# Who evacuates the transposed probabilities: one PSUM copy in two moved from ScalarE to VectorE, and the layer-norm pieces drained two heads later

## The chip, the cores and the metric

The kernel runs on all 8 cores of one Trainium2 chip. Each core takes one of the 8 batch entries; the cores exchange nothing. The metric is the device time of the slowest core in microseconds (us).

## What is computed

One post-layer-norm transformer layer on x of shape (8, 2048, 1024): windowed attention (16 heads of 64, causal, window 512) with a layer norm on every head's q and k, then an 8-bit quantized linear layer, each with a residual and a layer norm.

```python
qkv = x @ W_qkv + b_qkv                      # split into q, k, v; 16 heads of 64
q, k = layernorm(q, gq, bq), layernorm(k, gk, bk)   # per head
scores = q @ k.T / 8
scores = where((col > row) | (row - col >= 512), -inf, scores)
attn = softmax(scores) @ v
x1 = layernorm(x + attn @ W_out + b_out)
n  = x1 * rsqrt(mean(x1**2) + 1e-6)
q8 = clip(round(n * s), -128, 127) / s       # s = 127 / max|n|
out = layernorm(x1 + q8 @ (w_int8 * weight_scale).T + bias)
```

## The kernel before, in words

Each core works on 2048 rows in 16 tiles of 128 rows. All weights stay on the chip. A software pipeline of 21 rounds (`r`, `NR = NT + 5`) does in round r: the q, k and v projections of tile t = r, the attention of tile a = r-2, the output projection of tile p = r-3, the quantized layer of tile f = r-4, and the elementwise chains that follow p (as `pc = r-4`) and f (as `fc = r-5`). So rounds 2 and 3 have attention and no chains, round 4 has attention and the first chain only, rounds 5 to 17 have attention and both chains, and in rounds 16 and 17 the projections of q, k and v have ended.

Every engine runs its own list of instructions strictly in the order in which the program appended them (`S_.plan[engine]`); engines meet only at semaphores: `W(engine, sem, val)` appends a wait, `INC` an operation that counts a semaphore up when it is done. `FDV` (L172) and `FAC` (L176) append a one-column copy on VectorE and on ScalarE, called "fence" in the profile, whose end is what other engines wait for.

The attention of a tile is done in two halves of 8 heads (`attn_half`, half 0 with heads 0 to 7, half 1 with heads 8 to 15). Between the halves stand the k projection and, on VectorE, the normalization of q (L759 to L766), the statistics of k (L349 to L368) and the copy of the transposed keys into `kfm` (L786). For head h the program appends, in this order:

- `stage_scores` of h: TensorE multiplies q by the keys (L413 to L425) into one of two PSUM buffers, `big0` or `scp`; VectorE takes a maximum over 64 columns (L437, `negC`) and a fence; ScalarE takes the exponential (L444, `probs`); GpSimd multiplies it by the mask (L450).
- `stage_transpose` of h-2: TensorE transposes up to five 128x128 blocks of `probs` into the single PSUM buffer `ptp` (L186), which is then copied to `probsT`. This evacuation is done by VectorE for even heads (`pt_evac`, L196) and by ScalarE for odd heads (L465, followed by a fence). `G["ptev"]` remembers who evacuated last: the next transposes into `ptp` wait for it.
- `stage_av` of h-4: TensorE multiplies `probsT` by v into `avp` (L485); ScalarE copies the result to `araw` (L498). The single buffer `avp` makes each of these wait for the copy before it.
- `drain_chain(1)`: one piece of the elementwise chains.

After head 15 the two last transposes and the last four products follow, then VectorE divides by the sums (L524, L529).

The chains are lists of pieces in `pending_chain`. That of `pc` has seven: t1 (row sum, L551), t2 (sum of squares and small operations, L556 to L564, and the ScalarE square root chain), t3 (L582), t4 (L592 to L597), t5 (small operations, L605 to L619), t6 (L625 to L630) and t7 (L634 to L642). That of `fc` has four: ta (L652, L654), t1' and t2' (the same as t1 and t2) and tb (L663, and the store of the tile on the SyncE queue). In a round from 5 on there are thus 11 pieces, handed out one per head, and heads 11 to 15 have none. A piece stands in VectorE's list behind the head's maximum and evacuation and ahead of the next head's maximum.

Of the kernel before, what the change touches and what calls it, by code (L numbers as in the profile page):

```python
# [12 lines left out]
AF = mybir.ActivationFunctionType  # L13
# [16 lines left out]
class Sched:  # L30
# [13 lines left out]
    def W(self, eng, sem, val):  # L44
        if val and val > 0:
            h = self.sem[sem]
            self.trace[eng].append(("w", sem, val))
            self.plan[eng].append(lambda e, h=h, v=val: e.wait_ge(h, v))  # L48
# [14 lines left out]
    def INC(self, eng, sem, fn, k=1):  # L63
        self._self_edge(eng)
        self.cnt[sem] += k
        h = self.sem[sem]
        self.trace[eng].append(("i", sem, k))
        self.plan[eng].append(
            lambda e, fn=fn, h=h, k=k: fn(e).then_inc(h, k))
        return self.cnt[sem]  # L70
# [17 lines left out]
def build_nc():  # L88
# [19 lines left out]
    with st:  # L108
# [53 lines left out]
        ptb = ptp.ap()  # L162
# [4 lines left out]
        W, OP, INC = S_.W, S_.OP, S_.INC  # L167
        G = {"ptev": ("sDV", 0), "sqr": 0, "sqf": 0, "rysq": 0, "rsv": 0,
             "big0": 0, "big0k": "sDV", "big1": 0, "big1k": "sDV"}
# [5 lines left out]
        def FAC():  # L175
            return INC("scalar", "sAC", lambda e: e.activation(  # L176
                out=fence.ap()[:, 1:2], in_=cst.ap()[:, 0:1], func=AF.Square))
# [16 lines left out]
        def pt_evac(dst_ap, w, vPE):  # L194
            W("vector", "sPE", vPE)
            v = INC("vector", "sDV", lambda e, a=dst_ap, w=w: e.tensor_copy(  # L196
                out=a, in_=ptb[:, 0:w]))
            G["ptev"] = ("sDV", v)
            return v

        vS_const = 0
        for dst, src in [(mask4.ap(), d["mask4"]), (ident.ap(), d["ident"]),
# [8 lines left out]
            out=wqkv.ap().rearrange("p (k n) -> p k n", n=3 * E),  # L211
            in_=d["wqkv"].rearrange("(k p) n -> p k n", p=128)), 16)
        vG_wout = INC("gpsimd", "sWO", lambda e: e.dma_start(
            out=wout.ap().rearrange("p (k n) -> p k n", n=E),
# [238 lines left out]
        def stage_transpose(aa, h, vPL_m):  # L453
            u = aa * H + h
            nblk, w, _, _ = attn_geom(aa)
            pb = probs[u % 4].ap()
            vPE = transpose_group(
                lambda c, pb=pb: pb[:, c * 128:(c + 1) * 128],
                nblk, [("sPL", vPL_m)], "pT")
            vPE_tr_u[u] = vPE  # L460
            dst = probsT[u % 4].ap()[:, 0:w]
            if u % 2 == 1:
                W("scalar", "sPE", vPE_av_u.get(u - 4, 0))
                W("scalar", "sPE", vPE)
                INC("scalar", "sAC", lambda e, dst=dst, w=w: e.activation(  # L465
                    out=dst, in_=ptb[:, 0:w], func=AF.Copy))
                v = FAC()
                G["ptev"] = ("sAC", v)
                vDV_pt_u[u] = ("sAC", v)
            else:  # L470
                W("vector", "sPE", vPE_av_u.get(u - 4, 0))
                vDV_pt_u[u] = ("sDV", pt_evac(dst, w, vPE))
            expPEgate[u + 4] = vPE

        def stage_av(aa, h):
# [25 lines left out]
        def attn_half(aa, half):  # L501
            if half == 0:
                W("tensor", "sDV", vDV_qfm[aa])
                W("tensor", "sDV", vDV_kfm[aa])
                W("tensor", "sDV", vDV_vev[aa])
                G["attn_pend"] = []
            pend = G["attn_pend"]
            for h in range(8 * half, 8 * half + 8):
                m = stage_scores(aa, h)
                pend.append((h, m))  # L510
                if len(pend) >= 3:
                    hh, mm = pend.pop(0)
                    stage_transpose(aa, hh, mm)
                    if hh >= 2:
                        stage_av(aa, hh - 2)
                drain_chain(1)
            if half == 1:
                for hh, mm in pend:
                    stage_transpose(aa, hh, mm)
                for hh in range(H - 4, H):  # L520
                    stage_av(aa, hh)
                W("vector", "sAC", last_avev[aa * H + H - 1])
                a3 = araw.ap().rearrange("p (h c) -> p h c", c=65)
                INC("vector", "sDV", lambda e, a3=a3: e.reciprocal(  # L524
                    out=rcp[aa % 2].ap()[:, 0:16], in_=a3[:, :, 64:65]))
                rb_ = rcp[aa % 2].ap().rearrange(
                    "p (h u) -> p h u", u=1).broadcast_to([128, 16, 64])
                vno = INC("vector", "sDV", lambda e, a3=a3, rb_=rb_, aa=aa:
                          e.tensor_tensor(  # L529
                    out=attn[aa % 2].ap().rearrange("p (h c) -> p h c", c=64),  # L530
                    in0=a3[:, :, 0:64], in1=rb_, op=ALU.mult))
                G["anorm"] = vno
                vAC_attn_done[aa] = vno
# [3 lines left out]
        def drain_chain(n=None):  # L537
            k = len(pending_chain) if n is None else min(n, len(pending_chain))
            for _ in range(k):
                pending_chain.pop(0)()  # L540
# [418 lines left out]
```

How the kernel before makes its waits and increments, by code:

```python
    def W(self, eng, sem, val):  # L44
        if val and val > 0:
            h = self.sem[sem]
            self.trace[eng].append(("w", sem, val))
            self.plan[eng].append(lambda e, h=h, v=val: e.wait_ge(h, v))
# [14 lines left out]
    def INC(self, eng, sem, fn, k=1):  # L63
        self._self_edge(eng)
        self.cnt[sem] += k
        h = self.sem[sem]
        self.trace[eng].append(("i", sem, k))
        self.plan[eng].append(
            lambda e, fn=fn, h=h, k=k: fn(e).then_inc(h, k))
        return self.cnt[sem]
```

## Time and profile before

| what | value |
|---|---|
| time, median of 2 runs | 1887.78 us (1887.53 to 1888.02) |
| the profiled execution, its own time | 1885.52 us |
| its span on the slowest core (core 1) | 1883.8 us (all cores 1878.4 to 1883.8) |
| busy: TensorE, VectorE, ScalarE, GpSimd | 44%, 51%, 27%, 18% of the span |
| mean granted TensorE clock | 0.66 of full speed |

The profile is of one execution. The timeline gives for each instruction its start and its duration in us, and in brackets how long its engine had been idle and which engine's operation ended that. Line numbers are those of the kernel before.

### The profile page before, as it was taken

Reading aid. Unit: us, or ns where it says so; the run is one execution under the profiler, and the core shown is the slowest. Engines: PE = TensorE matmul, PEld = TensorE weight load, DVE = VectorE, ACT = ScalarE, POOL = GpSimd, SP = SyncE. Lnnn points to the kernel's source line nnn. Section 1 sums busy time; section 2 is a strip of 40 time slices with the busy share of each in tenths; the row PEclk is TensorE's granted clock in tenths of the full one; section 3 lists DMA queues with packets and bytes.
Section 4 is the critical chain, followed back from the end, with each engine's and each line's share of the span. In section 5 each row is a group of like instructions: output and inputs, shape, how many; then the busy total and the mean of one; then the engine's idle time right before and its main releaser. Section 6 shows DMA issues by size and latency. Waiting matters only on the chain.

```text
span 1883.8 us, 21143 instructions; the slowest of 8 cores (1878.4 to 1883.8 us)
## 1 busy us (share of the span) xinstructions
PE 833.7 (44%) x5096; PEld 428.0 (23%) x5096; DVE 965.8 (51%) x1873; ACT 511.8 (27%) x1105; POOL 336.5 (18%) x281
## 2 busy tenths in 40 slices
PE   0134555354444545344453543545454354444521
PEld 0021222121222222122322322232122222232300
DVE  2126553727455472744647365473736537455355
ACT  0001322322334132332413233241333324242311
POOL 0000111112213021221302122130222213132200
PEclk9996766666575756657575665757566575656565
DMA  9420000000101000010000101000010000000000
GB/s 153 91 67 6 1 6 6 12 6 1 29 1 29 1 7 23 1 29 1 25 4 1 28 1 29 1 23 6 1 28 1 23 1 23 1 23 1 23 11 23
DMA packets 11808, 35.11 MB, mean 19 GB/s; under 512 B 1322, under 2 KB 1450, under 8 KB 11690
## 3 DMA queue, kind: packets, MB, share of 16 engines
q0 software_dynamic: 4480, 12.59, 4.4%
q1 hardware_dynamic: 7210, 21.17, 3.3%
q8 instruction: 46, 0.75, 0.2%
q14 instruction: 72, 0.59, 0.1%
HBM read 37.97 MB, written 8.39 MB: 25 GB/s over the span
## 4 chain that ended last, share of the span: by engine, by line
DVE 45%; PE 25%; ACT 12%; issue 11%; DMA 3%; DVEq 2%; another core or an unknown queue 2%; ACTq 1%; POOL 0%; SPq 0%; POOLq 0%
PE big L331 7%; PE big L828 5%; PE ptp L186 4%; ACT probs L444 4%; PE big L858 3%; ACT probsT L465 3%; DMA rci<-w 2%; DVE probsT L196 2%; DVE fence L172 2%; DVE zzb L349 2%; DVE arena L359 2%; DVE negC L437 2%; DVE arena L351 2%; DVEq L48 2%; PE avp L485 2%
## 5 line engine op out<-in xcount | busy, mean ns | idle before, releaser
L450 POOL TENSOR_TENSOR probs<-probs,mask4s 128x640 bf16<-128x640 bf16 (+4 forms) x256 | 323.6, 1264 | 1285.2 <-ACT probs L444 1282.2
L186 PE MATMUL ptp<-idents,probs 128*128 128x128 bf16 x1120 | 160.3, 302 | 490.0 <-ACT fence L176 189.7
L331 PE MATMUL big<-wqkvb,xfm 128*128 128x512 bf16 x768 | 216.1, 445 | 58.3 <-DVE vtm L722 33.9
L186 PEld LDWEIGHTS ptp<-idents,probs 128*128 128x128 bf16 x1120 | 100.0, 129 | 575.9 <-issue 575.4
L828 PE MATMUL big<-woutb,afm 128*128 128x512 bf16 x256 | 91.6, 522 | 119.8 <-DVE afm L196 119.8
L444 ACT ACTIVATE probs<-scp,negC 128x640 bf16<-128x640 f32 (+4 forms) x128 | 93.0, 727 | 185.3 <-DVE fence L172 163.7
L485 PE MATMUL avp<-vtm,probsT 128*128 128x65 bf16 x1120 | 108.4, 243 | 60.8 <-ACT araw L498 57.6
L331 PEld LDWEIGHTS big<-wqkvb,xfm 128*128 128x128 bf16 x768 | 82.9, 112 | 179.9 <-issue 124.8
L356 ACT ACTIVATE sqqk<-zzb 128x1024 bf16<-128x1024 bf16 x32 | 33.8, 1057 | 318.3 <-DVE zzb L349 318.3
L196 DVE COPY probsT<-ptp 128x640 bf16<-128x640 bf16 (+4 forms) x128 | 57.6, 450 | 114.1 <-PE ptp L186 104.2
L444 ACT ACTIVATE probs<-big,negC 128x640 bf16<-128x640 f32 (+4 forms) x128 | 93.0, 727 | 63.7 <-DVE fence L172 53.4
L485 PEld LDWEIGHTS avp<-vtm,probsT 128*128 128x128 bf16 x1120 | 82.5, 129 | 83.5 <-issue 82.1
L870 ACT ACTIVATE hb<-big,lar 128x1024 f32<-128x1024 f32 x16 | 17.8, 1113 | 291.6 <-PE big L858 291.6
L465 ACT ACTIVATE probsT<-ptp 128x640 bf16<-128x640 bf16 (+4 forms) x128 | 81.5, 636 | 42.6 <-PE ptp L186 30.7
L349 DVE CAST zzb<-big 128x1024 bf16<-128x1024 f32 x32 | 39.2, 1225 | 89.6 <-PE big L338 88.2
L838 DVE TENSOR_TENSOR hb<-big,xres 128x1024 f32<-128x1024 f32 x16 | 19.6, 1225 | 110.6 <-PE big L832 110.6
L858 PE MATMUL big<-wfT,q8fm 128*128 128x512 bf16 x256 | 59.7, 387 | 37.4 <-DVE q8fm L196 37.4
L498 ACT ACTIVATE araw<-avp 128x65 bf16<-128x65 f32 x256 | 57.9, 226 | 59.8 <-PE avp L485 40.2
L172 DVE COPY fence<-cst 128x1 f32<-128x1 f32 x352 | 54.2, 154 | 37.9 <-DVE negC L437 2.1
L413 PE MATMUL big<-kfm,qfm 64*128 64x512 bf16 (+3 forms) x80 | 39.1, 489 | 71.2 <-ACT probs L444 70.8
L828 PEld LDWEIGHTS big<-woutb,afm 128*128 128x128 bf16 x256 | 28.8, 122 | 171.0 <-issue 162.4
L722 DVE CAST vtm<-big 128x512 bf16<-128x512 f32 x32 | 22.2, 694 | 68.8 <-PE big L338 66.9
(120 smaller groups left out, 1315.6 us busy)
## 6 DMA issues: line engine op xcount, KB each, us to landing
xres<-x SPq DMA_DIRECT2D x16, 512.0 KB, 4.5
out<-x1b SPq DMA_DIRECT2D x16, 512.0 KB, 2.9
wqkvb<-wqkv POOLq DMA_DIRECT2D x1, 6144.0 KB, 43.9
rci<-w SPq DMA_DIRECT2D x16, 256.0 KB, 2.8
xbf<-x POOLq DMA_DIRECT2D x16, 256.0 KB, 4.3
woutb<-wout POOLq DMA_DIRECT2D x1, 2048.0 KB, 56.0
mask4s<-mask SPq DMA_DIRECT2D x1, 160.0 KB
idents<-ident SPq DMA_DIRECT2D x1, 32.0 KB
```

What stands on the lines that cost most here:

```text
L172: return INC("vector", "sDV", lambda e: e.tensor_copy(out=fence.ap()[:, 0:1], in_=cst.ap()[:, 0:1]))
L186: fn = lambda e, src=src, c=c: e.transpose(ptb[:, c * 128:(c + 1) * 128], src, ident.ap())
L196: v = INC("vector", "sDV", lambda e, a=dst_ap, w=w: e.tensor_copy(out=a, in_=ptb[:, 0:w]))
L331: OP("tensor", lambda e, l=lhs, r=rhs, ps=ps, kk=kk: e.matmul(ps, l, r, start=(kk == 0), stop=False))
L349: vDV_cp = INC("vector", "sDV", lambda e, b=bigap: e.tensor_copy(out=zzb.ap(), in_=b))
L444: scb=scb: e.activation(out=pb[:, 0:w], in_=scb.ap()[:, 0:w], func=AF.Exp, bias=dstC, scale=1.0))
L450: e.tensor_mul(pb[:, 0:w], pb[:, 0:w], mask4.ap()[:, moff:moff + w]))
L465: INC("scalar", "sAC", lambda e, dst=dst, w=w: e.activation(out=dst, in_=ptb[:, 0:w], func=AF.Copy))
L485: fn = lambda e, pT=pT, j=j, vb=vb, last=(j == nblk - 1): e.matmul(avp.ap()[:, 0:65], pT[:, j * 128:(j + 1) * 128], vtm.ap()[:, vb:vb + 65 ...
L498: e.activation(out=dstA, in_=avp.ap()[:, 0:65], func=AF.Copy))
L828: OP("tensor", lambda e, l=l, rr=rr, n=n, kk=kk: e.matmul(big1.ap()[:, n * 512:(n + 1) * 512], l, rr, start=(kk == 0), stop=False))
L858: fn = lambda e, l=l, rr=rr, n=n, kk=kk: e.matmul(big1.ap()[:, n * 512:(n + 1) * 512], l, rr, start=(kk == 0), stop=(kk == NCH - 1))
```

## The change

Every evacuation of `ptp` into `probsT` is now done by VectorE, for odd heads as for even ones; ScalarE's copy and the fence behind it are gone for odd heads. And a piece of the chains is handed out only from head 2 of a tile on (`h` counts from 0 to 15 over both halves).

```diff
             dst = probsT[u % 4].ap()[:, 0:w]
-            if u % 2 == 1:
-                W("scalar", "sPE", vPE_av_u.get(u - 4, 0))
-                W("scalar", "sPE", vPE)
-                INC("scalar", "sAC", lambda e, dst=dst, w=w: e.activation(
-                    out=dst, in_=ptb[:, 0:w], func=AF.Copy))
-                v = FAC()
-                G["ptev"] = ("sAC", v)
-                vDV_pt_u[u] = ("sAC", v)
-            else:
-                W("vector", "sPE", vPE_av_u.get(u - 4, 0))
-                vDV_pt_u[u] = ("sDV", pt_evac(dst, w, vPE))
+            W("vector", "sPE", vPE_av_u.get(u - 4, 0))
+            vDV_pt_u[u] = ("sDV", pt_evac(dst, w, vPE))
             expPEgate[u + 4] = vPE
...
                     if hh >= 2:
                         stage_av(aa, hh - 2)
-                drain_chain(1)
+                if h >= 2:
+                    drain_chain(1)
```

Three places in the order of the engines show it, all in a round with both chains and five blocks. First VectorE at the end of half 0, from piece t6 on (`ry`, `rci`, `re`, `q8tm` are the chain's buffers); before:

```order
L625 TENSOR_SCALAR ry<-x1b,lar 128x1024
L628 CAST rci<-ry 128x1024
L630 TENSOR_TENSOR ry<-ry,rci 128x1024
L437 TENSOR_REDUCE negC<-big 128x1
L172 COPY fence<-cst 128x1
L196 COPY probsT<-ptp 128x640
L634 TENSOR_SCALAR re<-ry 128x1024
L636 TENSOR_SCALAR re<-ry 128x1024
L638 SCALAR_TENSOR_TENSOR ry<-rci,re 128x1024
L642 TENSOR_TENSOR q8tm<-ry,re 128x1024
L437 TENSOR_REDUCE negC<-scp 128x1
L172 COPY fence<-cst 128x1
```

The same place after the change, from the maximum of head 7 on, where t6 now stands in head 7 (its L617 to L622 are L625 to L630 before, L751 is L759):

```order
L437 TENSOR_REDUCE negC<-scp 128x1
L172 COPY fence<-cst 128x1
L196 COPY probsT<-ptp 128x640
L617 TENSOR_SCALAR ry<-x1b,lar 128x1024
L620 CAST rci<-ry 128x1024
L622 TENSOR_TENSOR ry<-ry,rci 128x1024
L751 TENSOR_TENSOR n_q<-zzb,arena 128x1024
```

Pieces t7 and ta, which stood ahead of the normalization of q, have left half 0, and head 7 has gained an evacuation. Next VectorE in heads 11 to 14 of half 1, where no piece was left before:

```order
L437 TENSOR_REDUCE negC<-scp 128x1
L172 COPY fence<-cst 128x1
L437 TENSOR_REDUCE negC<-big 128x1
L172 COPY fence<-cst 128x1
L196 COPY probsT<-ptp 128x640
L437 TENSOR_REDUCE negC<-scp 128x1
L172 COPY fence<-cst 128x1
L437 TENSOR_REDUCE negC<-big 128x1
```

After the change the pieces t2' (its last small operation stands first here) and tb (L655, before L663) are in heads 11 and 12, and every maximum is followed by an evacuation:

```order
L556 TENSOR_TENSOR lar<-lar 128x1
L172 COPY fence<-cst 128x1
L437 TENSOR_REDUCE negC<-big 128x1
L172 COPY fence<-cst 128x1
L196 COPY probsT<-ptp 128x640
L655 TENSOR_SCALAR x1b<-hb,lar 128x1024
L437 TENSOR_REDUCE negC<-scp 128x1
L172 COPY fence<-cst 128x1
L196 COPY probsT<-ptp 128x640
L437 TENSOR_REDUCE negC<-big 128x1
```

Last ScalarE in the same heads; before, every second exponential is followed by an evacuation and a fence:

```order
L444 ACTIVATE probs<-big,negC 128x640
L498 ACTIVATE araw<-avp 128x65
L444 ACTIVATE probs<-scp,negC 128x640
L465 ACTIVATE probsT<-ptp 128x640
L176 ACTIVATE fence<-cst 128x1
L498 ACTIVATE araw<-avp 128x65
```

and after the change it only alternates between the exponential and the small copy (L489 is L498 before):

```order
L444 ACTIVATE probs<-big,negC 128x640
L489 ACTIVATE araw<-avp 128x65
L444 ACTIVATE probs<-scp,negC 128x640
L489 ACTIVATE araw<-avp 128x65
L444 ACTIVATE probs<-big,negC 128x640
```

The order on TensorE, GpSimd and the two DMA queues is the same as before.

## Rows read from the trace of the kernel before

**Rows 1.** The page: the chain that ended last, shares of the span by engine.

```profile
DVE 45%; PE 25%; ACT 12%; issue 11%; DMA 3%; DVEq 2%; another core or an unknown queue 2%; ACTq 1%; POOL 0%; SPq 0%; POOLq 0%
```

**Rows 2.** Timeline of SyncE's queue: the stores of tiles, one a round.

```profile
704.89 0.34 SPq L669 DMA_DIRECT2D out<-x1b  x1
...
1592.81 0.34 SPq L669 DMA_DIRECT2D out<-x1b  x1
```

**Rows 3.** Windows: half 0 and half 1 of one round (us, busy, clock, DMA).

```profile
873.40:918.60 45.20, 16.09 (x111) 9.45 (x111) 34.85 (x61) 15.27 (x31) 11.49 (x8) 0.58 0.00 1
918.60:946.00 27.40, 15.78 (x152) 12.59 (x153) 10.02 (x29) 15.52 (x35) 11.74 (x9) 0.50 0.18 49
```

**Rows 4.** VectorE's evacuations, by tile: duration in ns, min/median/max.

```profile
L196 DVE COPY probsT<-ptp x128: 224/492/492, 206.5 to 1767.3; 128x640 bf16<-128x640 bf16 x96, 128x128 bf16<-128x128 bf16 x8, 128x256 bf16<-128x256 bf16 x8, 128x384 bf16<-128x384 bf16 x8
```

**Rows 5.** Timeline of half 0 in that round, VectorE with rows of TensorE and GpSimd.

```profile
873.43 0.22 DVE L437 TENSOR_REDUCE negC<-big 128x1 f32<-128x64 f32 x1
...
875.05 0.69 PE L425 MATMUL big<-kfm,qfm 64*128 64x128 bf16 x5 [6.96 <-ACT probs L444]
...
876.76 0.69 PE L186 MATMUL ptp<-idents,probs 128*128 128x128 bf16 x5 [1.02 <-POOL probs L450]
...
885.17 1.22 DVE L592 TENSOR_REDUCE lar<-ry 128x1 f32<-128x1024 f32 x1 [3.41 <-ACT ry L589]
...
895.17 2.23 DVE L630 TENSOR_TENSOR ry<-ry,rci 128x1024 f32<-128x1024 f32 x1
...
898.69 0.69 DVE L634 TENSOR_SCALAR re<-ry 128x1024 bf16<-128x1024 f32 x1
...
903.94 0.23 DVE L437 TENSOR_REDUCE negC<-scp 128x1 f32<-128x64 f32 x1
...
905.63 1.39 POOL L450 TENSOR_TENSOR probs<-probs,mask4s 128x640 bf16<-128x640 bf16 x1 [5.00 <-ACT probs L444]
905.86 2.24 DVE L654 TENSOR_TENSOR hb<-hb,x1b 128x1024 f32<-128x1024 f32 x1
908.20 1.23 DVE L759 TENSOR_TENSOR n_q<-zzb,arena 128x1024 bf16<-128x1024 bf16 x1
...
918.62 0.23 DVE L437 TENSOR_REDUCE negC<-big 128x1 f32<-128x64 f32 x1
```

**Rows 6.** Timeline of all engines in two heads without a piece, half 1.

```profile
930.86 0.49 DVE L196 COPY probsT<-ptp 128x640 bf16<-128x640 bf16 x1 [1.57 <-PE ptp L186]
930.89 0.71 PE L425 MATMUL scp<-kfm,qfm 64*128 64x128 bf16 x5
...
931.78 0.23 DVE L437 TENSOR_REDUCE negC<-scp 128x1 f32<-128x64 f32 x1 [0.43 <-PE scp L425]
...
932.47 0.79 ACT L444 ACTIVATE probs<-scp,negC 128x640 bf16<-128x640 f32 x1 [1.10 <-DVE fence L172]
...
933.35 0.70 ACT L465 ACTIVATE probsT<-ptp 128x640 bf16<-128x640 bf16 x1
...
934.49 0.69 PE L186 MATMUL ptp<-idents,probs 128*128 128x128 bf16 x5 [1.32 <-ACT fence L176]
```

**Rows 7.** Timeline of the end of half 1: last maximum, transposes, products, division.

```profile
936.28 0.23 DVE L437 TENSOR_REDUCE negC<-scp 128x1 f32<-128x64 f32 x1 [0.43 <-PE scp L425]
...
940.49 0.69 PE L186 MATMUL ptp<-idents,probs 128*128 128x128 bf16 x5 [0.81 <-DVE probsT L196]
...
942.90 0.43 PE L485 MATMUL avp<-vtm,probsT 128*128 128x65 bf16 x5 [1.44 <-ACT araw L498]
...
945.03 0.43 PE L485 MATMUL avp<-vtm,probsT 128*128 128x65 bf16 x5 [0.63 <-ACT araw L498]
...
946.01 0.25 DVE L524 RECIPROCAL rcp<-araw 128x16 f32<-128x16 bf16 x1 [5.66 <-ACT araw L498]
```

**Rows 8.** Timeline of VectorE in round 3 (two blocks): maxima two heads apart.

```profile
292.06 0.23 DVE L437 TENSOR_REDUCE negC<-scp 128x1 f32<-128x64 f32 x1 [0.35 <-PE scp L413]
...
295.32 0.23 DVE L437 TENSOR_REDUCE negC<-scp 128x1 f32<-128x64 f32 x1 [0.36 <-PE scp L413]
```

## The prediction

> **What bounds the kernel now.** I read the chain of waits first. VectorE has 45% of it, TensorE 25%, ScalarE 12% [rows 1]: no engine is full, and the end is set by engines that hand work to each other. So I looked for the length of a round and for what ends last inside one. The stores of finished tiles come once a round; eight rounds take 1592.81 - 704.89 = 887.9 us, 111.0 us each [rows 2]. The windows split one such round in three: half 0 of the attention takes 45.2 us, half 1 27.4 us, and 38.4 us are left for projections, the quantized layer and the statistics of q, which the change doesn't touch [rows 3].
>
> In half 0 VectorE is busy 34.85 us with 61 instructions [rows 3]. Between two of them lie about 0.1 us, so some 41 of the 45.2 us are taken: VectorE is the bound there, and what it really waits for is under 4 us, 3.41 of it in one place, for ScalarE's square in piece t4 [rows 5]. In half 1 it is busy 10.0 of 27.4 us [rows 3]. There, in the heads that have no piece, the time goes in a ring. The evacuation at 930.86 follows transposes that began 0.69 + 0.18 earlier, at 929.99, and the next of that kind begin at 934.49: 4.50 us for two heads. ScalarE's part of it is visible: the exponential of an even pair runs 932.47 to 933.26, the odd evacuation stands behind it in ScalarE's list until 933.35 although its transposes are long done, and TensorE, which has only one transpose buffer, waits 1.32 us for the fence behind it [rows 6].
>
> **The change part by part.** The three parts are the pieces that move, the evacuations that VectorE gains, and the waits that go or come. I follow the round of rows 5 to 7 through, from the first maximum at 873.43.
>
> *Half 0.* Shifted by two heads, pieces t7 and ta leave half 0. t7 runs from 898.69 to 903.94, 5.25 us; ta fills 903.94 + 0.59 (maximum and fence with their gaps) to 908.20, 3.67 us [rows 5]. That is -8.92 us in the place where VectorE is the bound. It gains the evacuations of heads 1, 3 and 5: 0.492 us each [rows 4] and a gap of 0.10, so 3 x 0.59 = +1.77. The waits: without t1 and t2 in heads 0 and 1, VectorE idles until the scores of head 2, which come at 875.05 + 0.69 + 0.18 = 875.92 while it is free at 874.60, and then until the transposes of head 0 are done, 876.76 + 0.69 + 0.17 = 877.62 against 876.50; that makes 1.32 + 1.12 = 2.44 [rows 5]. The wait in t4 (3.41 less the gap of 0.10) shrinks: the square has to follow the exponential of its head (0.79 [rows 6]) and one small copy, by ScalarE's durations 2.65 us behind the fence where it was 3.41, and an evacuation of 0.59 now fits in it, so 1.96 are left. Two waits of about 0.3 (in t2 and at the evacuation of head 4) go, and t2 no longer meets the mask (0.33). Waits: 2.44 + 1.96 = 4.40 against 0.30 + 3.31 + 0.34 = 3.95, so +0.45. Sum: -8.92 + 1.77 + 0.45 - 0.33 = -7.0. Half 1 would begin at 911.6 in place of 918.62.
>
> The k projection and its cast are the other way in which half 0 could end late; by the same walk TensorE can start it at about 894 and needs 6 us, and VectorE gets to it at 905, so it stays covered.
>
> *Half 1.* Heads 8 to 12 are now VectorE's alone: 5 x (0.58 + 0.59) for maximum, fence and evacuation = 5.85; 0.32 for the first transposes, which wait for the shared buffer; t7 4.94 and ta 3.09 (both end at a mask's end, so the evacuation ahead of them is partly absorbed: below), t1' 1.33, t2' 2.56, tb 1.0. That is 19.1 us, against heads 8 to 10 with the same three last pieces before. Heads 13 to 15 have no piece. What they cost: from the start of a maximum to the start of that head's transposes, 876.76 - 873.43 = 3.33 us at least (fence, exponential, mask) [rows 5]; from the start of scores to that of the maximum 931.78 - 930.89 = 0.89 [rows 6]; and between scores of h and transposes of h lie two head periods and one set of scores, 0.71. So a period is (3.33 + 0.89 - 0.71)/2 = 1.75 us in place of 4.50/2 = 2.25. With somewhat more for head 15, the maximum of head 15 comes at 911.6 + 19.1 + 3.7 = 934.4. Before it was 936.28.
>
> *The tail.* From that maximum to the division it took 946.01 - 936.28 = 9.73 us [rows 7]. Now the last transposes can start 3.3 us behind it in place of 4.21, and the second of the four last products no longer waits for ScalarE's evacuation: the spacing was 942.90 - 940.98 = 1.92 for the first (it began 0.49 behind 940.49) and is (945.03 - 942.90)/2 = 1.07 for the others [rows 7], so 0.85 go. 9.73 - 0.9 - 0.9 = 7.9. The division comes at 942.2 in place of 946.01: half 1 takes 30.6 us, +3.2, and the round -3.8 us.
>
> How sure is each term? The copies: an odd evacuation on VectorE is the same instruction as the even one, whose median and maximum agree (0.492) [rows 4]; this term is firm. What an edit costs where its cover is gone: if the transposes are not done when VectorE reaches the evacuation, it waits, as it does for 1.57 us in the row at 930.86 [rows 6], and the next maximum is queued behind it, with ScalarE and GpSimd behind that. In heads with pieces the transposes had a whole piece (0.8 to 5 us) to run in. The bounds of the round are then: -7.0 + 1.2 = -5.8 below, if half 1 loses only what VectorE's sum demands, and -7.0 + 8.92 = +1.9 above, if half 1 pays all that half 0 saves. The walk's -3.8 lies between, nearest to the rows.
>
> One row deserves a closer look, since evacuations shift pieces against the mask. L654 takes 2.24 us, where ta's other addition, over as many columns, has 905.86 - 904.53 = 1.33 with its gap. It began at 905.86, inside the mask that GpSimd ran from 905.63 to 907.02, and ended 1.08 us behind the mask's end; L630 with its 2.23 us looks the same [rows 5]. The Trainium skill (SBUF — State Buffer, "Who interferes with whom") says that the two engines share a port pair as an exclusive lock, so a VectorE instruction with two SBUF inputs, or a copy in a two-port mode, is fully blocked while GpSimd works; the trace agrees. By that rule a later start of a piece costs nothing when it is absorbed in the block, and a copy out of PSUM isn't blocked, as the even evacuations' constant 0.492 also shows. Had I taken pieces t7 and ta at their full 5.25 and 3.67, the round would be at -2.9 in place of -3.8.
>
> *Other rounds.* Rounds 5 to 17 hold both chains: 13 x 3.8 = 49.4 us (rounds 16 and 17 lack the q normalization between the halves, which is the same before and after). Rounds 2 to 4 have narrower heads and none or seven of the pieces. In round 3 two heads take 3.26 us [rows 8], 1.63 a head; by the ring above, with narrower operations, some 1.3 are left, so about 0.3 x 14 heads + 1 for the tail = 5. Bounds are 0 and 7 a round; I take 4.1 each, 12.3 us together. Sum: -61.7 us. Against the profiled execution that is 1885.5 - 61.7 = 1823.8; the median of the runs lies 2.3 us above that execution, so 1826.
>
> **The rivals.**
>
> A. *Only half 0 gains.* The heads without pieces don't get faster (another ring, over the small copy to `araw` and the products, could hold them at 2.25 us), and the tail keeps its 9.73 us. Then the maximum of head 15 comes at 930.7 + 3 x 2.25 less what was queued, about 934.4, and the division at 944.1: -1.9 a round, 13 x 1.9 + 12 = 37 us, 1851. For it: TensorE is at its lower level in half 1 (0.50 granted, 1.2 GHz) [rows 3] and the durations of a head there, 0.71 + 0.69 + 0.43 = 1.83 [rows 6, 7], are more than 1.75, though they overlap. Against it: the 1.32 us wait in rows 6 is ScalarE's alone.
>
> B. *TensorE's clock rises.* The gaps in half 1 close and the granted clock goes from 0.50 [rows 3] to full. Scores, transposes and products of a head shrink from 1.83 to some 1.2 us (an estimate: half at best, 0.9); of heads 13 to 15, tail and the projection behind it that takes perhaps 3 us a round, so 1826 - 39 = 1787. Against it: heads 8 to 12 get slower, not denser.
>
> C. *Slower: VectorE becomes the only evacuator and pays in full.* Place: VectorE's list between the evacuation of head h-2 and the maximum of head h+1. Price: 128 x (0.45 mean + 0.10) = 70 us, if nothing is given back, 1888 + 70 = 1958. It decides from the point where VectorE has no idle time left to take 8 evacuations (4.7 us) a round; half 0 has under 4 [rows 3]. Against it: 17 us of half 1 are idle now, and the pieces that leave half 0 are worth more than what comes in. The Trainium skill speaks for this rival: TensorEngine Tiling (Array Packing), "Performance Considerations", advises to use both ScalarE and VectorE for PSUM evacuation. By that rule the change goes the wrong way. The trace agrees only in half 0; in half 1 sharing costs more than it brings, since ScalarE's copy takes 0.70 against 0.49, with a fence behind it, and queues behind an exponential [rows 4, 6].
>
> D. *The change does nothing*: the shift of pieces and the evacuations cancel, 1888.
>
> **How the numbers follow.** My forecast, 1826 with its own spread of 1805 to 1845, gets 0.66; A 0.16; B 0.08; C 0.04; D 0.06. A measurement of this kernel tells about 2% from no change, so faster means below 1850. That holds for the forecast, for B and for a good part of A: 0.77. Same: the rest of A, D: 0.19. Slower: C, 0.04. The range runs from 1800 to 1868: it takes in A and leaves out B, C, D.
>
> **What would show each step.** In the profile after: VectorE's 256 evacuations at 0.49 us for 640 columns and no ScalarE row for `probsT`; rounds of about 107.2 us; half 0 near 38 us and half 1 near 30.6; two heads without pieces in 3.5 to 3.8 us; the wait in t4 below 2.1 us; a new VectorE idle of about 2.4 us in heads 0 to 2; 7.9 us from the last maximum to the division. I am wrong if half 1 takes over 34 us (then the moved pieces push everything behind them), if half 0 is above 41 (then another engine bounds it), or if the untouched 38.4 us change, which only the clock could do.

## The result, and the profile after

The kernel after takes 1850.15 us (median of 11 runs, 1849.38 to 1850.98); before it is 1887.78 us (10 runs). The ratio of the means is 0.979, with a 95% interval of 0.9765 to 0.9815 (one of the ten runs before took 1910.35 us; by the medians it is 0.980). That is 37.6 us less by the medians, 2.0 to 2.1%. The prediction counted a time below 1850 as told from no change, and this one is at that edge. The forecast was 1826, 61.7 us less: the direction was right and the size was off by 24 us. The time lies inside the range, and almost on the number of rival A (1851), though not for A's reason, as the parts below show.

The page of the kernel after: the chain that ended last, and two groups of instructions (out<-in, count, then busy us and mean ns of one, then idle time before them and its releaser).

```profile
DVE 48%; PE 25%; issue 12%; ACT 6%; DMA 3%; POOL 2%; DVEq 2%; another core or an unknown queue 2%; ACTq 0%; POOLq 0%; SPq 0%
...
L450 POOL TENSOR_TENSOR probs<-probs,mask4s 128x640 bf16<-128x640 bf16 (+4 forms) x256 | 334.1, 1305 | 1237.4 <-ACT probs L444 1228.5
...
L196 DVE COPY probsT<-ptp 128x640 bf16<-128x640 bf16 (+4 forms) x256 | 115.2, 450 | 87.6 <-PE ptp L186 66.1
```

Against [rows 1], ScalarE's share of the chain is halved (12% to 6%) and VectorE's has grown from 45 to 48%. All 256 evacuations are VectorE's, at the mean of 450 ns that its 128 had. GpSimd's mask has a longer mean than before, 1305 ns against 1264 on the page before; that is the first trace of what the sum got wrong.

The stores of tiles, answering to [rows 2]:

```profile
698.52 0.34 SPq L661 DMA_DIRECT2D out<-x1b  x1
...
1568.75 0.34 SPq L661 DMA_DIRECT2D out<-x1b  x1
```

Eight rounds take 870.2 us, 108.8 each in place of 111.0. The forecast was 107.2. The same round as in [rows 3], with half 0, half 1 and the rest up to the next first maximum (us, then busy time of TensorE, its weight loads, VectorE, ScalarE, GpSimd, then TensorE's clock, DMA share and GB/s):

```profile
857.88:895.87 37.99, 15.18 (x110) 9.27 (x111) 27.17 (x59) 12.57 (x25) 11.25 (x8) 0.59 0.00 1
895.87:927.27 31.40, 16.35 (x153) 12.35 (x153) 20.27 (x40) 10.98 (x25) 12.69 (x9) 0.50 0.15 43
927.27:966.93 39.66, 21.99 (x105) 8.95 (x105) 15.22 (x21) 2.74 (x5) 0.00 (x0) 0.76 0.00 1
```

Half 0 takes 37.99 us (forecast 38.2), half 1 31.40 (forecast 30.6), and the part that the change doesn't touch 39.66. One round says little of the last; the means over rounds 6 to 15 (5 to 14 for the rest), measured for each kernel from the timeline of the core that its profile shows, between the first maximum of half 0, that of half 1 and the division, are the yardstick for all that follows. The time is the median of the runs. The ratios given further down are each against the kernel before as it ran beside that kernel (1885.5 to 1886.3 us), so they differ a little from ratios of this column:

| kernel | half 0 | half 1 | rest | time, us |
|---|---|---|---|---|
| before | 45.0 | 27.5 | 38.4 | 1887.8 |
| after | 38.3 | 31.5 | 38.9 | 1850.2 |
| evacuations alone | 45.2 | 23.6 | 38.4 | 1827.8 |
| shift alone | 38.5 | 33.7 | 38.6 | 1884.6 |
| after, no mask in heads 8, 9 | 38.3 | 29.5 | 38.0 | 1811.5 |
| before, odd heads 9 to 15 on VectorE | 44.7 | 23.5 | 38.4 | 1824.3 |
| after, short mask | 36.2 | 29.5 | 38.6 | 1787.3 |
| before, short mask | 41.9 | 27.0 | 38.5 | 1838.4 |
| evacuations alone, short mask | 42.0 | 23.0 | 38.5 | 1779.6 |
| after, empty heads 2, 3 for 0, 1 | 39.1 | 31.6 | 38.9 | 1852.8 |
| after, two pieces in heads 2, 3 | 46.7 | 23.6 | 38.9 | 1852.0 |
| after, one delay of 1.8 us | 38.4 | 31.6 | 38.8 | 1848.5 |
| after, one delay of 3.6 us | 38.2 | 31.7 | 38.9 | 1848.7 |
| odd heads 9 to 15 on VectorE, short mask | 41.6 | 22.4 | 39.6 | 1775.9 |

### The profile page after: what moved, and what is told of

It is laid out like the page before. It is cut to its first block, busy times and chain, and to the rows that moved or that the text cites. A ratio compares the mean times of both kernels' runs of the same rounds, so it can differ in the third digit from the quotient of the medians.

```text
span 1847.8 us, 20839 instructions; the slowest of 8 cores (1838.5 to 1847.8 us)
## 1 busy us (share of the span) xinstructions
PE 837.5 (45%) x5048; PEld 427.2 (23%) x5096; DVE 1012.8 (55%) x2001; ACT 404.8 (22%) x849; POOL 347.0 (19%) x281
## 4 chain that ended last, share of the span: by engine, by line
DVE 48%; PE 25%; issue 12%; ACT 6%; DMA 3%; POOL 2%; DVEq 2%; another core or an unknown queue 2%; ACTq 0%; POOLq 0%; SPq 0%
PE big L331 8%; PE big L820 5%; DVE probsT L196 4%; PE ptp L186 4%; PE big L850 3%; DMA rci<-w 2%; DVE fence L172 2%; DVE negC L437 2%; PE avp L476 2%; DVE zzb L349 2%; ACT probs L444 2%; DVE lar L548 2%; DVE arena L359 2%; POOL probs L450 2%; DVEq L48 2%
## 5 line engine op out<-in xcount | busy, mean ns | idle before, releaser
L450 POOL TENSOR_TENSOR probs<-probs,mask4s 128x640 bf16<-128x640 bf16 (+4 forms) x256 | 334.1, 1305 | 1237.4 <-ACT probs L444 1228.5
L196 DVE COPY probsT<-ptp 128x640 bf16<-128x640 bf16 (+4 forms) x256 | 115.2, 450 | 87.6 <-PE ptp L186 66.1
L820 PE MATMUL big<-woutb,afm 128*128 128x512 bf16 x240 | 85.0, 516 | 126.3 <-DVE afm L196 126.3
L476 PEld LDWEIGHTS avp<-vtm,probsT 128*128 128x128 bf16 x1120 | 76.8, 125 | 97.2 <-issue 96.0
L489 ACT ACTIVATE araw<-avp 128x65 bf16<-128x65 f32 x256 | 58.1, 227 | 96.4 <-PE avp L476 78.2
L437 DVE TENSOR_REDUCE negC<-big 128x1 f32<-128x64 f32 (+1 forms) x128 | 28.3, 221 | 44.5 <-PE big L418 11.0
```

The lines of the kernel that those rows point to most:

```text
L437: e.tensor_reduce(out=dstC, in_=scb.ap()[:, cst:cst + cw], axis=AX.X, op=ALU.max, negate=True))
L450: e.tensor_mul(pb[:, 0:w], pb[:, 0:w], mask4.ap()[:, moff:moff + w]))
L476: fn = lambda e, pT=pT, j=j, vb=vb, last=(j == nblk - 1): e.matmul(avp.ap()[:, 0:65], pT[:, j * 128:(j + 1) * 128], vtm.ap()[:, vb:vb + 65 ...
L489: e.activation(out=dstA, in_=avp.ap()[:, 0:65], func=AF.Copy))
L820: OP("tensor", lambda e, l=l, rr=rr, n=n, kk=kk: e.matmul(big1.ap()[:, n * 512:(n + 1) * 512], l, rr, start=(kk == 0), stop=False))
```

## Experiments

The question was where 24 us of the expected gain had gone, and which part of the change earns the rest.

**One part at a time.** First the change was cut in two. Evacuations alone: the kernel after with

```diff
-                if h >= 2:
-                    drain_chain(1)
+                drain_chain(1)
```

> Only the evacuations move to VectorE; pieces are handed out from head 0 on, as before. Theory (the ring over ScalarE was the cost of half 1, VectorE's sum is that of half 0): half 0 stays near 45.5 us (three evacuations more, the wait in t4 shorter), half 1 falls from 27.5 to about 24 us, a round gains 3 us, the whole some 40 us: about 1848, as fast as the kernel after. Rival (the shift of the pieces is what pays): half 1 stays at 27.5, half 0 rises by the three evacuations, and the time is 1890 to 1910.

It takes 1827.8 us, ratio 0.9688 [0.9673, 0.9702]: faster than the kernel after by 22 us, and 20 us below the 1848 of the theory. Half 1 fell to 23.6. Rounds 2 to 4, which the expectation had not counted apart, bring 13 of the 58 us. The rival is out. Here are the heads without pieces of half 1 in this kernel, VectorE, from a maximum to the division:

```profile
904.13 0.22 DVE L437 TENSOR_REDUCE negC<-big 128x1 f32<-128x64 f32 x1 [0.46 <-PE big L425]
905.07 0.49 DVE L196 COPY probsT<-ptp 128x640 bf16<-128x640 bf16 x1 [0.46 <-PE ptp L186]
...
907.71 0.22 DVE L437 TENSOR_REDUCE negC<-big 128x1 f32<-128x64 f32 x1 [0.43 <-PE big L425]
...
909.28 0.22 DVE L437 TENSOR_REDUCE negC<-scp 128x1 f32<-128x64 f32 x1 [0.43 <-PE scp L425]
...
917.31 0.25 DVE L515 RECIPROCAL rcp<-araw 128x16 f32<-128x16 bf16 x1 [3.35 <-ACT araw L489]
```

Two heads take 907.71 - 904.13 = 3.58 us, 1.79 a head, where the prediction had 1.75 and the kernel before 2.25 [rows 6]. From the last maximum to the division it is 8.03 us (7.9 predicted, 9.73 before [rows 7]). In the mean of rounds 6 to 15 the four periods from head 11 to head 15 are 1.67 us each, against 2.25 before. The ring over ScalarE was read rightly as the bound before. One more row of the kernel before shows the queue in it, the transposes of an odd head:

```profile
931.54 0.72 PE L186 MATMUL ptp<-idents,probs 128*128 128x128 bf16 x5
```

They are done by about 932.44 (0.72 + 0.18 after their start), and ScalarE's copy starts at 933.35 [rows 6], 0.91 us later, behind the exponential. From the start of that copy to the next transposes it is 934.49 - 933.35 = 1.14 us. Which share of the gain is the queue and which the shorter copy on VectorE, no run separates.

Shift alone: the kernel before with

```diff
-                drain_chain(1)
+                if h >= 2:
+                    drain_chain(1)
```

> Only the shift: pieces from head 2 on, odd evacuations stay on ScalarE. Theory: half 0 falls by 5 to 6.5 us to about 39, half 1 rises by 4 to 6 us to about 32.5, since the two moved pieces cost 8.9 us there and only part of it fills idle time of VectorE: a round gains 0 to 2 us, 1865 to 1888. Rival (the shift pays): 1850 or less, and evacuations alone bring nothing.

1884.6 us, 0.9991 [0.9981, 1.0]: the same as before. Half 0 falls by 6.5 us and half 1 rises by 6.2. On top of the evacuations the shift costs 22 us: half 0 falls by 6.8 and half 1 rises by 7.9. So the two parts don't add: 58.5 + 1.7 us (each against the kernel before beside it, 1886.3) is not 37.6. In the kernel before, heads 11 to 15 had idle VectorE time to give to the moved pieces, and they were slow for another reason; once the evacuations have made them fast and filled them with copies, the pieces cost nearly their full length, 7.9 of 8.9 us.

**What the shift costs.** Two more kernels take the shift apart. The first has empty heads elsewhere, and t7 and ta still in half 1:

```diff
-                if h >= 2:
+                if h not in (2, 3):
                     drain_chain(1)
```

> The kernel after, with pieces handed out in heads 0 and 1 again and none in heads 2 and 3 instead, so that t7 and ta are in half 1 as in the kernel after. Theory (the shift loses because t1 and t2 covered the 2.4 us in which VectorE waits for the first scores and transposes): half 0 falls from 38.3 to about 36.5, half 1 stays at 31.5, about 1825, no slower than evacuations alone. Rival (the shift loses because the moved pieces cost more in half 1 than in half 0): no gain against the kernel after, 1850.

1852.8 us, 0.9824 [0.981, 0.9839], and half 0 at 39.1 against 38.3. The theory fell: t1 and t2 do not cover heads 0 and 1 any better than other pieces would. The trace shows the same idle time in its new place, between heads 2 and 4:

```profile
862.85 0.49 DVE L196 COPY probsT<-ptp 128x640 bf16<-128x640 bf16 x1 [0.42 <-PE ptp L186]
863.58 0.22 DVE L437 TENSOR_REDUCE negC<-big 128x1 f32<-128x64 f32 x1 [0.24 <-PE big L425]
...
865.28 0.49 DVE L196 COPY probsT<-ptp 128x640 bf16<-128x640 bf16 x1 [1.23 <-PE ptp L186]
865.88 1.91 DVE L574 TENSOR_SCALAR x1b<-hb,lar 128x1024 f32<-128x1024 f32 x1
```

0.42, 0.24 and 1.23 us of waiting, and 1.91 us for t3, which takes 0.81 elsewhere. GpSimd is at its mask from 862.77 to 867.24 there, and t3 ends 0.55 us after that. The second kernel keeps heads 0 and 1 empty but moves no piece into half 1:

```diff
                 if h >= 2:
-                    drain_chain(1)
+                    drain_chain(2 if h in (2, 3) else 1)
```

> The kernel after, with no piece in heads 0 and 1 but two in each of heads 2 and 3, so that t7 and ta are back in half 0 and only the empty heads are left of the shift. Theory (the shift loses the idle time that opens in half 0 wherever two heads have no piece, some 2 us, and the moved pieces cost in half 1 nearly what they save in half 0): half 0 about 47, half 1 23.6, a round 2 us over evacuations alone: about 1850, like the kernel after. Rival (the price lies in half 1, where t7 and ta are dearer): as evacuations alone, 1828.

1852.0 us, 0.9825 [0.981, 0.9839]; half 0 is 46.7 and half 1 23.6 as with evacuations alone. So a kernel that moves nothing into half 1 is 24 us slower all the same. Half 0 is 1.5 us a round longer than with evacuations alone, some 19 us over 13 rounds, and that is the price of the empty heads. The other 0.5 us a round lies in the rest, which no edit touches; it goes with TensorE's clock (the part that nobody touched, below), and whether the empty heads cause it is not shown. Moving t7 and ta as well, which is the step from this kernel to the kernel after, takes 8.3 us out of half 0 and puts 7.9 into half 1, with hardly any change in time (1852.0 against 1850.2, intervals of the ratio that overlap). The idle time in the first heads of this kernel:

```profile
856.98 0.23 DVE L437 TENSOR_REDUCE negC<-big 128x1 f32<-128x64 f32 x1
...
859.47 0.22 DVE L437 TENSOR_REDUCE negC<-big 128x1 f32<-128x64 f32 x1 [1.42 <-PE big L425]
...
861.18 0.49 DVE L196 COPY probsT<-ptp 128x640 bf16<-128x640 bf16 x1 [1.23 <-PE ptp L186]
```

Less a gap in each, 1.42 + 1.23 is 2.45 us. By the sums over half 0 of rounds 6 to 15, the other waits are together 0.7 us shorter than with evacuations alone (the one in t4 is 1.43 us against 1.73), and instructions are busy 0.3 us less, which leaves the 1.5.

**The mask and the moved pieces.** Next the 0.9 us a round by which half 1 exceeded the walk. VectorE and GpSimd in heads 8 and 9 of the kernel after, where t7 (L626 to L634) and ta (L644, L646) now stand:

```profile
897.37 0.69 DVE L626 TENSOR_SCALAR re<-ry 128x1024 bf16<-128x1024 f32 x1
...
898.17 1.69 DVE L628 TENSOR_SCALAR re<-ry 128x1024 bf16<-128x1024 f32 x1
...
902.63 0.23 DVE L437 TENSOR_REDUCE negC<-scp 128x1 f32<-128x64 f32 x1
...
903.81 1.23 DVE L644 TENSOR_TENSOR hb<-hb,fbrep 128x1024 f32<-128x1024 f32 x1
905.14 2.23 DVE L646 TENSOR_TENSOR hb<-hb,x1b 128x1024 f32<-128x1024 f32 x1
907.47 0.23 DVE L437 TENSOR_REDUCE negC<-big 128x1 f32<-128x64 f32 x1
```

and GpSimd in the same heads:

```profile
897.55 1.76 POOL L450 TENSOR_TENSOR probs<-probs,mask4s 128x640 bf16<-128x640 bf16 x1 [14.09 <-ACT probs L444]
904.31 1.98 POOL L450 TENSOR_TENSOR probs<-probs,mask4s 128x640 bf16<-128x640 bf16 x1 [5.00 <-ACT probs L444]
```

The prediction let the mask start and end on time and shortened the pieces, 4.94 for t7 and 3.09 for ta. But L626 and L644 were already running when the mask came. The mask took 1.76 and 1.98 us in place of 1.39, it ended later by that difference, and the VectorE instruction behind was stretched as before: t7 is 5.26 us long and ta 3.66, the same as in half 0 of the kernel before (5.25 and 3.67). To see whether the lengths really come from the mask, heads 8 and 9 lost it, so that the attention of these two heads is left unmasked:

```diff
+            if h in (8, 9):
+                w = 1
             return INC("gpsimd", "sPL", lambda e, pb=pb, w=w, moff=moff:
                        e.tensor_mul(pb[:, 0:w], pb[:, 0:w],
```

> The kernel after, with GpSimd's mask cut to one column in heads 8 and 9 (these heads are left unmasked). Theory (pieces t7 and ta are stretched by about 1 us each because one of their instructions waits for GpSimd's mask to end): t7 falls from 5.26 to about 4.3 us, ta from 3.66 to about 2.7, half 1 from 31.5 to about 29.6, the whole by 25 us against the kernel after. Rival (half 1 is long for another reason, such as a late transpose): both pieces keep their length, half 1 stays at 31.5 and the time at 1850.

```profile
884.66 0.69 DVE L628 TENSOR_SCALAR re<-ry 128x1024 bf16<-128x1024 f32 x1
885.46 0.69 DVE L630 TENSOR_SCALAR re<-ry 128x1024 bf16<-128x1024 f32 x1
...
890.10 1.23 DVE L646 TENSOR_TENSOR hb<-hb,fbrep 128x1024 f32<-128x1024 f32 x1
891.43 1.22 DVE L648 TENSOR_TENSOR hb<-hb,x1b 128x1024 f32<-128x1024 f32 x1
```

The same instructions take 0.69 and 1.22 us where they took 1.69 and 2.23; half 1 is 29.5, 2.0 us less, and the time 1811.5, 0.9602 [0.9588, 0.9617]. That is 38.7 us below the kernel after, where 26 were expected: the halves account for 26 us and the rest of the round, which this kernel doesn't touch either, for most of the remainder (38.0 against 38.9). So the part of the gain beyond 26 us goes with TensorE's clock, as below, and was not foreseen. The Trainium skill (SBUF — State Buffer, "Who interferes with whom") has both sides of this: whichever of the two engines issues first keeps the shared ports for its whole instruction, so order decides who blocks. The trace agrees, for VectorE at 2.23 us and for GpSimd at 1.98. The prediction used only one side of the rule.

**A shorter mask.** The mask's columns are all ones in the three middle blocks of five. So it can be cut to two blocks of 128 columns, or one where there are fewer than five, with the same result:

```diff
+            if aa >= 4:
+                pv = pb.rearrange("p (b c) -> p b c", c=128)[:, 0:5:4, :]
+                mv = mask4.ap().rearrange("p (b c) -> p b c", c=128)[:, 0:5:4, :]
+            else:
+                pv = pb[:, w - 128:w]
+                mv = mask4.ap()[:, 512:640]
-                       e.tensor_mul(pb[:, 0:w], pb[:, 0:w],
-                                    mask4.ap()[:, moff:moff + w]))
+                       e.tensor_mul(pv, pv, mv))
```

In the kernel after:

> The kernel after, with GpSimd's mask only over the first and last block of five (the three between are all ones in the mask; with fewer blocks only the last). 256 columns take 0.67 us in round 3, against 1.39 for 640. Theory (lock between GpSimd and VectorE's pieces, and a head period set by maximum, exponential, mask and transposes): pieces t6, t7 and ta each lose 0.5 to 1 us, half 0 falls from 38.3 to 37, half 1 from 31.5 to about 28.5, the whole by 50 to 60 us against the kernel after: about 1795. Rival (the mask is hidden outside the two heads of e6): no more than e6's gain, 1811 or above.

1787.3 us, 0.9473 [0.9459, 0.9487], 63 us less than after: half 0 -2.2, half 1 -2.0, the rest -0.3. In the kernel before:

> The kernel before with the same short mask. Theory: in its heads without pieces the ring goes over ScalarE, not over the mask, so only the stretched instructions in t6, t7, ta and t2 shrink, 2 to 4 us a round and nothing in the free heads: 1840 to 1855. Rival (the mask sets the free heads' period too): half 1 falls from 27.5 below 24 and the time below 1830.

1838.4 us, 0.9746 [0.9731, 0.976]. Most of it is in half 0 (45.0 to 41.9). Half 1 falls from 27.5 to 27.0, all of it in head 9, which has piece t2'; the periods of the heads without pieces stay as they were, so in the kernel before the mask was not in the ring that set them. With evacuations alone:

> All evacuations on VectorE, pieces from head 0 on, short mask. Theory: the effects add, since they lie in different places: half 0 from 45.2 to about 43, half 1 from 23.6 to 21 to 22, 4 to 5 us a round less than evacuations alone: 1765 to 1780. Rival (in the free heads the products' ring over ScalarE's small copy takes over): half 1 stays at 23, 1795.

1779.6 us, 0.9434 [0.9418, 0.9449]. Half 0 falls as before by 3.2, half 1 only by 0.6, to 23.0 and not to 21 or 22. The mask takes 0.67 us in place of 1.39, and yet heads 12 and 13 need 891.16 - 887.81 = 3.35 us for the 3.58 above:

```profile
887.81 0.23 DVE L437 TENSOR_REDUCE negC<-big 128x1 f32<-128x64 f32 x1 [0.46 <-PE big L425]
887.97 0.67 POOL L457 TENSOR_TENSOR probs<-probs,mask4s 128x256 bf16<-128x256 bf16 x1 [1.10 <-ACT probs L444]
...
891.16 0.22 DVE L437 TENSOR_REDUCE negC<-big 128x1 f32<-128x64 f32 x1 [0.43 <-PE big L425]
```

Even that is more than the heads gain in the mean, where the next period is longer in turn: from head 11 to head 15 it is 6.62 us against 6.68. The 0.6 us are the tail behind the last maximum, 7.58 against 8.14. So the mask doesn't set the heads without pieces in this kernel. The windows over the last three periods, evacuations alone and then with the short mask, show what is nearly full:

```profile
904.13:909.28 5.15, 4.80 (x46) 3.79 (x47) 2.61 (x10) 3.06 (x6) 4.18 (x3) 0.50 0.45 148
887.81:892.88 5.07, 5.03 (x48) 3.64 (x46) 2.61 (x9) 3.21 (x7) 2.04 (x4) 0.50 0.46 150
```

TensorE is busy 4.80 of 5.15 us and 5.03 of 5.07, at its lower level (0.50 granted, 1.2 GHz), and in the second window its groups of matmuls follow each other with no idle time shown. The ends of matmuls are modelled in a profile, so this is a reading and no experiment; but it makes TensorE's own work the bound of these heads, rather than the mask or ScalarE's small copy.

**Sharing the evacuations where each engine has time.** The kernel before, with ScalarE keeping the odd heads 1 to 7 only:

```diff
-            if u % 2 == 1:
+            if u % 2 == 1 and h < 9:
```

> The kernel before, with odd heads 9 to 15 alone evacuated by VectorE: ScalarE keeps the odd evacuations of heads 1 to 7, which fall where VectorE has pieces to do, and pieces are handed out from head 0 on. Theory (an evacuation costs 0.59 where VectorE is the bound and gains where it is not): half 0 45.0 as before, half 1 about 23.5, 4 us less a round, some 52 us less in all: about 1836, faster than the kernel after. Rival (it is all the same which engine copies, or a mixture of both loses by the change between them): 1850 or more.

1824.3 us, 0.9671 [0.9655, 0.9687], against 0.9688 [0.9673, 0.9702] with all on VectorE: the intervals overlap. It is 12 us below the expectation, which again left out rounds 2 to 4. Against all on VectorE, half 0 gains 0.4 us a round, where three copies of 0.59 are saved; with ScalarE's copies the wait for its square in t4 is 3.41 us in place of 1.73, which is nearly as much. With the short mask on top:

> Short mask, ScalarE evacuating odd heads 1 to 7 and VectorE the rest, pieces from head 0 on. Theory: half 0 0.4 us below that with all evacuations on VectorE, about 41.6, half 1 the same at 23.0: 1772 to 1777 against 1779.6, at the edge of what can be told. Rival: ScalarE's copy makes TensorE wait in half 0 and the time is 1785 or more.

1775.9 us, 0.9411 [0.9396, 0.9427], the fastest kernel of the study and 4% below the kernel after; whether it beats its neighbour at 0.9434 is at the edge of the intervals. Half 1 came out at 22.4 and not 23.0, so that the halves are 1.0 us a round below that neighbour; the rest is 1.1 longer on the core shown and takes it back. In three of the ten rounds the stretch from the copy of `q8fm` to that of `xfm` takes 6.6 us in place of 5.07, by the same kind of lengthening as in the next part.

**The part that nobody touched.** From after one division to the next first maximum it is 38.4 us before and 38.9 after. The main difference is one stretch, from the start of the first cast of v to that of the cast of q: in rounds 6 to 15 of these two kernels it takes 5.96 or 7.65 us, nothing between. Here are both kinds in the kernel after, TensorE in the q projection of two rounds:

```profile
414.83 3.61 PE L331 MATMUL big<-wqkvb,xfm 128*128 128x512 bf16 x16 [1.81 <-DVE vtm L714]
...
954.75 5.30 PE L331 MATMUL big<-wqkvb,xfm 128*128 128x512 bf16 x16 [1.88 <-DVE vtm L714]
```

and the windows around them (columns as above):

```profile
413.00:419.50 6.50, 4.69 (x29) 2.08 (x28) 1.73 (x3) 0.00 (x0) 0.00 (x0) 1.00 0.00 0
954.70:961.20 6.50, 6.45 (x30) 2.58 (x32) 0.44 (x1) 0.00 (x0) 0.00 (x0) 0.74 0.00 0
```

With the clock at full (2.4 GHz) the 16 products take 3.61 us; where it falls to 1.2 GHz partway, with the engine idle 1.9 us before in both rounds, they take 5.30. Of the ten rounds 6 to 15 five have the long form before, nine after, four with evacuations alone, ten in the kernel with two pieces in heads 2 and 3 and none with no mask in heads 8 and 9, on the core that each profile shows. (The expectations below count rounds 3 to 14, of which the first two take 7.5 to 8.0 us and were left out.) Four long ones more are 4 x 1.69 / 10 = 0.68 us a round; the stretch up to the output projection gives 0.16 back, which leaves the 0.5. To see whether the position in time decides, the kernel after was delayed once, at round 5:

```diff
                 G["attn_pend"] = []
+                if aa == 3:
+                    for _ in range(7):      # 14 in the other kernel
+                        FDV()
```

> The kernel after, with 7 more fences (0.26 us each with the gap, 1.8 us in all) on VectorE once, ahead of head 0 in round 5, and nowhere else. In the kernel after the q projection takes 7.65 us in 8 of 12 rounds and 5.96 in the others, in the kernel before 7.65 in 4 of 12. Theory (which of the two it takes hangs on where the round falls in time against the moments at which TensorE's clock is changed; rounds of 109.05 us keep falling badly): a single delay moves all later rounds, most of them take 5.96, the time falls by up to 8 x 1.7 = 13 us in spite of the delay: about 1840. Rival (the clock falls because of what TensorE does inside the new round): the 8 long ones stay and the time is 1852.

> As the kernel with 7 fences, but 14 (3.6 us). Theory: the rounds fall elsewhere again, and the number of long q projections differs from that with 7, so the time isn't 1.8 us above it: if the first delay brought the good position, this one loses it, about 1853. Rival: 1.8 us above the kernel with 7 fences.

1848.5 and 1848.7 us, 0.9802 [0.9788, 0.9817] and 0.9801 [0.9787, 0.9816]. Both expectations missed. The long form comes 7 and 8 times in place of 8, so the delay bought no good position; nor did the kernels get slower by 1.8 and 3.6 us. In the first, round 4, into whose end the delay falls, was longer by 1.8 us (96.86 against 95.06 us), and round 5 was shorter by 1.4 (103.96 against 105.32): the q projection behind it took its short form, where it takes the long one without the delay. With 3.6 us the time that was lost had been made up when round 11 began, and later rounds differ again by up to 3 us. What sets the form of a round stays open: one delay moved it in some rounds and did not move the total. Its size is known, 1.7 us a time.

## Why the prediction was right, and where it was not

*What bounds the kernel* held: VectorE in half 0, the ring over ScalarE in half 1. Half 0 came out at 38.3 us against 38.2 in the walk, with the waits at 1.42 and 1.22 us where 1.32 and 1.12 stood without their gaps, and t4's wait 2.05 with its gap where 1.96 stood without. The price of an evacuation, 0.49 and a gap, held for all with 640 columns. The tail held: 8.03 us in the round shown (919.24 to 927.27) against 7.9. The last two periods before it, from head 13 to head 15, took 919.24 - 915.89 = 3.35 us, below the 3.5 to 3.8 that were to show the step. There the number was near for a reason that is in part luck: the walk built the period of 1.75 us on the mask, and the short mask left these heads as they were (6.62 us for four periods against 6.68). TensorE's work at its lower level, which stood only as an argument for rival A, is what nearly fills them.

So the mechanism was right in its main parts, and the gain came out at 0.61 of the forecast. The terms that were mis-sized, for the 61.7 - 37.6 = 24 us:

- "t7 4.94 and ta 3.09 (both end at a mask's end, so the evacuation ahead of them is partly absorbed)". They took 5.26 and 3.66, 0.89 us more, and half 1 rose by 4.05 us a round, not 3.2: 11 us over 13 rounds. The run with no mask in heads 8 and 9 shows where it comes from, 4.26 and 2.66. The text named the alternative, -2.9 a round for pieces at their full length; the halves of the kernel after give 38.3 + 31.5 against 45.0 + 27.5, -2.6.
- Half 0 fell by 6.7 and not by 7.0 us: 4 us.
- "38.4 us are left ..., which the change doesn't touch". Untouched in the program, but 0.5 us longer a round on the core shown, some 7 us in all with rounds 2 to 4. The prediction named the clock as the only thing that could do it, and gave it no term and no spread.
- Rounds 2 to 4 were taken at 12.3 us; their halves gave 11.7.

These come to 11 + 4 + 7 + 1 = 23 us. The rivals: A had the right number by the wrong way, since the heads without pieces and the tail did get faster. Its number doesn't follow from its condition either: with periods of 2.25 us the maximum of head 15 comes at 930.7 + 6.75 = 937.5, and no row gives the 3 us "less what was queued"; the round would then be 1.2 us longer and not 1.9 shorter. Nor does the 0.77 for a time below 1850 hold a good part of A, since the forecast and B make 0.74 of it and A's own number lies above 1850. B did not happen (0.50 granted in half 1 before and after). C had beside it the advice to use both engines for the evacuation of PSUM (the Trainium skill, TensorEngine Tiling (Array Packing), "Performance Considerations"). Here all on VectorE beats half and half by 3%, and the placed mixture is the same as all on VectorE. Half and half is 0.2 us a round better in the crowded half and costs 3.9 in the other, so the advice without a condition does not hold for this kernel. D is out.

What the prediction didn't ask is what each half of the change is worth alone. It summed both in one walk, and the walk gave the moved pieces 8.9 us in half 0, which looked like the main gain. The shift is in fact a loss of 22 us on top of the evacuations: what it takes out of half 0 comes back in half 1, since VectorE is the bound of the heads with pieces in both once it evacuates everything; two heads of half 0 are left idle; and some 5 to 7 us of the 22 are the clock's, for which the shift may or may not be the cause. The forecast thus put one gain together from a larger gain and a loss, and that their sum fell inside the range is partly luck.

## What to carry to other kernels

When a change has two edits, walk each alone before the two together: work moved from a stage that an engine bounds is a gain only if the place that it goes to still has idle time of that engine after the other edit. Before a copy is shared between engines, look for what stands ahead of it in each list: in this kernel a faster copy and a shorter queue beat sharing the load. And where two engines share a port, an overlap can stretch either of them, so a piece moved against it is counted at full length unless a row shows otherwise. A difference below 1% between two variants may be the clock's in a part that neither touches.

## What the runs showed of the hardware that I had not expected

- GpSimd's 640-column mask takes 1.39 us alone and, in the kernel after, up to 1.98 us when a VectorE instruction with two inputs is already running; the VectorE instruction behind it then takes 2.23 in place of 1.23 us. Both pay. Cutting the mask to 256 columns, 0.67 us, is worth 48 to 63 us of 1828 to 1888 in the three kernels in which nothing else was changed with it.
- The same 16 products take 3.61 or 5.30 us in rounds of one execution, as TensorE's clock falls in them or not, and a delay of 1.8 or 3.6 us ahead of one round did not show in the time (1848.5 and 1848.7 us against 1850.2). Over ten rounds the long form comes anywhere from never to ten times in kernels that don't touch this stage, which is up to 17 us a kernel.
